# The inverse square root for x1, in the query-group loop: its Newton steps on GpSimd instead of VectorE

## The chip, the cores and the metric

One core of one Trainium2 chip runs the whole program. The metric is the device time of one execution in microseconds; lower is better.

## What is computed

The input x is [16, 16, 48, 128]: 16 batches of 768 tokens with 128 channels. Three blocks follow one another.

```
x = x + conv_attention(group_norm(x))          # 8 heads of 16, 768 x 768 scores, two biases, causal in t
t = t + additive_attention(layer_norm(t))      # tanh(A_i + B_j + b1), weighted by w2; softmax; times V
t = t + moe(layer_norm(t))                     # 8 experts, top 2, capacity 3840, gelu
layer_norm(v) = (v - mean(v)) / sqrt(var(v) + 1e-5)      # over the 128 channels of a token
```

The change is in the first `layer_norm`, that of x1 (the output of the first block). The kernel makes 1/sqrt(var + 1e-5) from a bit-trick seed and three Newton steps: y = y * (1.5 - 0.5 * var * y * y). A batch has 768 variances, held as 128 partitions x 6 numbers.

## The kernel before, in words

The work on batches is a software pipeline. Each batch goes through five stages (`STAGES`): pre (group norm, q, k, v), max (row maxima of the scores), mid (scores, weighted values, project, x1 and its layer norm), add (the additive attention) and end (second layer norm, gate, sending rows to experts). A pass holds one stage of each of up to five batches, and has 24 ticks. Pass p has batch p in add, p+1 in mid, p-1 in end. Passes -3 to 0 are written out, 1 to 12 are a hardware loop of two passes a turn (`passes`), 13 to 15 are written out again. The expert stage runs after all passes, from about 2090 us.

Every engine walks the same ticks in its own order of instructions, written out by hand; semaphores join them. TensorE, VectorE, ScalarE each have a `body(ps)`; the parts that matter here:

- **GpSimd** (`body`, L817): in tick q it first makes the sums of query group q (`sums`, L791): three instructions of 128x768 on `hidden` (L803), with a drain ahead of the second and third (ahead of the first too in ticks 7 to 18), the last of them raising `sums_ready`. It waits first for `logits_added` (L798), that is, until TensorE has used the `hidden` slot of four groups ago, and for group 0 for `ab_ready`. In ticks 18 to 23 and 0 to 5 it then sends one block of rows to the experts (`send`, L812: an indirect DMA whose descriptors GpSimd makes, L814).
- **ScalarE** (L889): in tick q it takes the exponentials of two score banks (L879), every fourth tick those of the logits (L886, which waits for VectorE's `logit_bias`), then waits for `sums_ready` of group q and takes the tanh of the sums (L902) and of a fourth part that it sums by itself (L906).
- **TensorE** (L1098): in tick q+1 it adds the logits of group q (`add_logits`, L978), fills score banks (L948, L951), weighs values (L964) and fills the three banks of `ring`: row maxima (L1052), and in ticks 20 and 21 the transposes of the normed x1 (L1037) and the products B and A (L1066), which wait for VectorE's copies of those transposes (L1291).
- **VectorE** (L1425): reads the ring banks in the order of their filling, and between the four slots of a tick has the small work. For x1: statistics in ticks 16 and 17; `norm_scale(0, k)` (L1205) with k = 0 (add 1e-5, seed: L1210, L1126) in tick 17 slot 2, and k = 1, 2, 3 (a Newton step each: L1129, L1131, L1133) in tick 17 slot 3 and tick 18 slots 1 and 3; then `normed` (L1216) for three blocks in tick 19 slot 1 and three in slot 3, which raises `x1n_ready`.

The same `norm_scale` serves the second layer norm (which = 1, ticks 4 to 6); the change leaves it.

## Time and profile before

| | |
|---|---|
| median of three runs | 2384.56 us (2372.84 to 2385.24) |
| the profiled execution | 2384.78 us, span 2383.0 us |
| TensorE busy | 2053.2 us, 86% of the span |
| VectorE busy | 1675.7 us, 70% |
| ScalarE busy | 1683.2 us, 71% |
| GpSimd busy | 1461.3 us, 61% |
| granted TensorE clock, mean | 0.951 of full speed |

The profiled execution took 1.8 us more than its span, and lies within 0.3 us of the median. The busy shares are averages over the passes and the expert stage. Semaphore waits and drains are not counted as busy; in the timelines they show as idle time ahead of an instruction, in brackets, with what ended it ("issue" when the profile shows no releaser).

### The profile page before, as it was taken

How to read it: one execution, taken by the hardware profiler on the slowest of the kernel's cores; microseconds unless marked ns; L12 is line 12 of the kernel's file. 1: busy time of each engine (PE TensorE's matmuls, PEld its weight loads, DVE VectorE, ACT ScalarE, POOL GpSimd, SP SyncE). 2: the span in 40 equal slices, each digit the busy share in tenths (PEclk: the TensorE clock that was granted, in tenths of full speed). 3: DMA queues.
4: the chain of work that ended last, by engine and by line, in shares of the span. 5: the costliest groups of instructions: out<-in, count | busy, mean ns of one | idle time of the engine just before them, and what ended most of it. 6: DMA issues, size and time to landing. Idle time of an engine off the chain costs nothing.

```text
span 2383.0 us, 56242 instructions
## 1 busy us (share of the span) xinstructions
PE 2053.2 (86%) x17665; PEld 1122.5 (47%) x17665; DVE 1675.7 (70%) x4534; ACT 1683.2 (71%) x1933; POOL 1461.3 (61%) x1525
## 2 busy tenths in 40 slices
PE   2889999989998999989998999999999977549986
PEld 1344444444444444444444444444444433338775
DVE  5787787787878787868786878787877665324433
ACT  5238787877887788778787878788878977613332
POOL 3006576656666656565666666666657877627777
PEclk7799999999999999999999999999999988869998
DMA  4546322322222223222323131313131000025553
GB/s 94 89 86 128 95 48 61 55 62 56 61 56 61 56 59 57 58 60 51 66 50 68 42 70 29 81 32 77 32 65 32 12 6 4 7 54 90 84 86 37
DMA packets 157499, 137.99 MB, mean 58 GB/s; under 512 B 24665, under 2 KB 149814, under 8 KB 157104
## 3 DMA queue, kind: packets, MB, share of 16 engines
q1 hardware_dynamic: 119376, 109.87, 22.5%
q0 software_dynamic: 23824, 16.85, 5.2%
q10 hardware_dynamic: 13968, 7.30, 1.2%
q8 instruction: 154, 2.52, 0.5%
q14 instruction: 177, 1.45, 0.2%
HBM read 82.68 MB, written 54.52 MB: 58 GB/s over the span
## 4 chain that ended last, share of the span: by engine, by line
PE 39%; DVE 22%; issue 13%; DVEq 9%; POOL 6%; ACT 4%; POOLq 3%; DMA 2%; SPq 0%; another core or an unknown queue 0%; ACTq 0%
PE logits L978 12%; DVE max_halves L1261 4%; POOL out_dram L583 4%; PE ring L1052 3%; PE av_bank L964 3%; POOLq L802 3%; PE ring L1074 3%; PE ring L1066 3%; PE scores L948 3%; PE scores L951 2%; ACT hidden L902 2%; DVE logit_bias L1447 2%; POOL hidden L803 2%; PE ring L1071 2%; DVEq L1448 2%
## 5 line engine op out<-in xcount | busy, mean ns | idle before, releaser
L803 POOL TENSOR_SCALAR hidden<-b_rep,a_cols 128x768 f32<-128x768 f32 x1152 | 1057.1, 920 | 765.6 <-issue 302.9
L902 ACT ACTIVATE hidden<-hidden 128x2304 f32<-128x2304 f32 x384 | 816.1, 2125 | 16.4 <-POOL hidden L803 16.4
L978 PE MATMUL logits<-hidden,w_shifted 128*32 128x384 f32 x6144 | 591.6, 504 | 65.3 <-ACT hidden L906 30.9
L879 ACT ACTIVATE probs<-scores 128x512 f32<-128x512 f32 (+1 forms) x768 | 391.9, 545 | 325.6 <-PE scores L951 320.9
L1261 DVE TENSOR_REDUCE max_halves<-ring 128x1 f32<-128x384 f32 (+4 forms) x896 | 471.3, 550 | 115.8 <-PE ring L1052 114.2
L906 ACT ACTIVATE hidden<-b_rep,a_cols 128x768 f32<-128x768 f32 x384 | 358.4, 933 | 0.0
L1052 PE MATMUL ring<-k_max,q_max 112*128 112x384 bf16 (+4 forms) x1024 | 296.0, 319 | 34.8 <-DVE max_halves L1261 25.9
L978 PEld LDWEIGHTS logits<-hidden,w_shifted 128*32 128x32 f32 x6144 | 164.0, 110 | 314.9 <-issue 246.7
L948 PE MATMUL scores<-bias_q,onehot_k 112*128 112x512 bf16 (+1 forms) x768 | 276.4, 360 | 4.8 <-ACT probs L879 1.8
L951 PE MATMUL scores<-q_parts,k_parts 98*128 98x256 bf16 (+1 forms) x1536 | 277.3, 262 | 0.0
L814 POOL DMA_INDIRECT expert_rows<-rows,slots x198 | 199.5, 1007 | 64.2 <-issue 32.7
L964 PE MATMUL av_bank<-probs,v_aug 128*32 128x256 f32 (+1 forms) x3072 | 224.8, 364 | 6.3 <-DVE headsT_raw L1433 6.1
L951 PEld LDWEIGHTS scores<-q_parts,k_parts 98*128 98x128 bf16 x1536 | 153.3, 100 | 116.8 <-issue 20.1
L1052 PEld LDWEIGHTS ring<-k_max,q_max 112*128 112x128 bf16 x1024 | 91.0, 99 | 245.2 <-issue 95.0
L886 ACT ACTIVATE probs<-logits,logit_bias 128x768 f32<-128x768 f32 x96 | 86.6, 902 | 132.7 <-DVE logit_bias L1449 127.9
L1074 PE MATMUL ring<-v,probs1T 128*128 128x128 f32 x1152 | 153.2, 284 | 21.8 <-DVE max_halves L1261 13.0
L1074 PEld LDWEIGHTS ring<-v,probs1T 128*128 128x128 f32 x1152 | 139.5, 195 | 41.4 <-DVE max_halves L1261 19.7
L510 ACT ACTIVATE hidden<-scores,eb1T 128x384 f32<-128x384 f32 x80 | 46.2, 581 | 132.2 <-PE scores L471 129.6
L1319 DVE COPY probs1T<-ring 128x384 f32<-128x384 f32 x192 | 102.6, 548 | 34.5 <-PE ring L1071 34.2
L964 PEld LDWEIGHTS av_bank<-probs,v_aug 128*32 128x32 f32 x3072 | 70.3, 109 | 103.8 <-issue 80.8
L482 PEld LDWEIGHTS logits<-probs,hidden 128*128 128x128 f32 x960 | 113.4, 192 | 12.1 <-issue 1.7
L482 PE MATMUL logits<-probs,hidden 128*128 128x128 f32 x960 | 113.7, 275 | 1.6 <-DVE gn_small L552 1.6
(262 smaller groups left out, 2585.8 us busy)
## 6 DMA issues: line engine op xcount, KB each, us to landing
qk_parts<-qk_parts_sb SPq DMA_DIRECT2D x16, 1152.0 KB, 4.7
q_parts<-qk_parts SPq DMA_DIRECT2D x192, 96.0 KB, 3.2
k_parts<-qk_parts SPq DMA_DIRECT2D x192, 96.0 KB, 4.3
q_max<-qk_parts SPq DMA_DIRECT2D x96, 96.0 KB
k_max<-qk_parts SPq DMA_DIRECT2D x96, 96.0 KB
expert_rows<-clear_row ACTq DMA_DIRECT2D x9, 792.0 KB, 5.0
x_in<-in_x_dram SPq DMA_DIRECT2D x96, 64.0 KB
x<-in_x_dram SPq DMA_DIRECT2D x96, 64.0 KB
```

The lines of the kernel that those rows point to most:

```text
L482: last = mm(logits[:, n % 2, P * b_:P * b_ + P], gelu_out[n % 2][:, j, P * b_:P * b_ + P], down_w[r][:, j, :], start=(j == 0), stop=(j == 3))
L803: last = g.tensor_scalar(hidden[:, q % SLOTS, o, :], b_rep[:, side], 1.0, a_cols[:, side, a_col(q, o):a_col(q, o) + 1], ALU.mult, ALU.add)
L879: s.activation(probs0[:, d % 3, 2 * pair:2 * pair + 2, 0:n_], scores[:, pair].rearrange("p (j l) -> p j l", j=2)[:, :, 0:n_], ACT.Exp) \
L902: s.activation(hidden[:, t % SLOTS, 0:3, :], hidden[:, t % SLOTS, 0:3, :], ACT.Tanh)
L906: s.activation(hidden[:, t % SLOTS, 3, :], b_rep[:, side], ACT.Tanh, bias=a_cols[:, side, col:col + 1]).then_inc(tanh_done, 1)
L948: mm(bank[:, :, 0:n_], onehot_k[:], bias_q[:, h:h + 2, q0 - P * kb:q0 - P * kb + n_], start=True, stop=False, skip_group_check=True)
L951: last = mm(bank[:, j, 0:n_], k_parts[0:98, h + j, P * kb:P * kb + P], q_parts[0:98, h + j, q0:q0 + n_], start=False, stop=True, skip_grou ...
L964: last = mm(av_bank[32 * g:32 * g + 32, q0 - lo:q0 - lo + n_], v_aug[:, side, kb, 4 * quad + g, :], probs0[:, d % 3, g, 0:n_], start=(kb = ...
L978: last = mm(logits[32 * g:32 * g + 32, half, 0:HALF], w2_shifted[:, k, :], hidden[:, q % SLOTS, g, HALF * half:HALF * half + HALF], start= ...
L1052: last = mm(bank[:, keys * j:keys * j + keys], q_max[:, h + j, P * qb:P * qb + P], k_max[:, h + j, lo:lo + keys], start=True, stop=True)
L1074: last = mm(bank[:, 0:P], probs1T[:, P * kb:P * kb + P], v1[:, ps.side(stage), kb, :], start=(kb == 0), stop=(kb == TB - 1))
L1261: v.tensor_reduce(max_halves[:, h:h + n_, part], bank[:, 0:n_ * keys].rearrange("p (h k) -> p h k", h=n_), AX.X, ALU.max, negate=True).the ...
```

## The change

GpSimd makes the three Newton steps for x1. VectorE still makes var + 1e-5 and the seed in tick 17, and the seed raises the new semaphore `x1_seeded`. GpSimd, in its tick 19, behind the three sums and ahead of the row send of that tick, waits for `x1_seeded` and issues twelve operations on 128x6 numbers, four to a step, with a drain between dependent ones; the last raises `x1_scaled`. VectorE waits for `x1_scaled` ahead of the first `normed` in tick 19, where it had a drain. VectorE's nine Newton operations and their drains are gone.

```
+SCALE_AT = 19
...
+            def norm_scale(ps):
+
+                var, y, tmp = (ln_small[:, 0, r, 0:TB] for r in range(3))
+                pool.wait_ge(x1_seeded, ps.batch("mid") + 1)
+                pool.sem_inc(pool_passed, 1)
+                for step in range(3):
+                    g.tensor_tensor(tmp, y, y, ALU.mult)
+                    pool.drain()
+                    g.tensor_tensor(tmp, tmp, var, ALU.mult)
+                    pool.drain()
+                    g.tensor_scalar(tmp, tmp, -0.5, 1.5, ALU.mult, ALU.add)
+                    pool.drain()
+                    last = g.tensor_tensor(y, y, tmp, ALU.mult)
+                    if step == 2:
+                        last.then_inc(x1_scaled, 1)
+                    else:
+                        pool.drain()
...
                     if ps.has("add"):
                         sums(ps, t)
+                    if t == SCALE_AT and ps.has("mid"):
+                        norm_scale(ps)
                     if ps.has("end"):
...
-                    rsqrt_seed(y, var)
+                    last = rsqrt_seed(y, var)
+                    if which == 0:
+                        last.then_inc(x1_seeded, 1)
...
-                            if t == 17 and slot >= 2:
-                                norm_scale(0, slot - 2)
-                            if t == 18 and slot in (1, 3):
-                                norm_scale(0, 2 + slot // 2)
-                            if t == 19 and slot in (1, 3):
-                                if slot == 1:
-                                    dve.drain()
-                                for tb in range(3 * (slot // 2), 3 * (slot // 2) + 3):
+                            if t == 17 and slot == 2:
+                                norm_scale(0, 0)
+                            if (t, slot) in ((19, 1), (19, 3)):
+                                half = slice(0, 3) if (t, slot) == (19, 1) else slice(3, 6)
+                                if half.start == 0:
+                                    dve.wait_ge(x1_scaled, ps.batch("mid") + 1)
+                                for tb in range(half.start, half.stop):
                                     last = normed(0, x1_, x1n, tb)
-                                if slot == 3:
+                                if half.start:
                                     last.then_inc(x1n_ready, 1)
```

GpSimd's instructions from tick 19 to tick 20 of a pass of the loop, before (L803 are the sums, L814 the row send, `x3` three in a row):

```order
99 L803 TENSOR_SCALAR hidden<-b_rep,a_cols 128x768 x3
100 L814 DMA expert_rows<-rows,slots 15360x132
101 L798 REGISTER_ALU
102 L803 TENSOR_SCALAR hidden<-b_rep,a_cols 128x768 x3
103 L814 DMA expert_rows<-rows,slots 15360x132
104 L798 REGISTER_ALU
```

and with the change (the sums are L806 there, the send L835; L816 to L822 are a Newton step):

```order
124 L806 TENSOR_SCALAR hidden<-b_rep,a_cols 128x768 x3
125 L813 REGISTER_ALU
126 L816 TENSOR_TENSOR ln_small<-ln_small 128x6
127 L818 TENSOR_TENSOR ln_small<-ln_small 128x6
128 L820 TENSOR_SCALAR ln_small<-ln_small 128x6
129 L822 TENSOR_TENSOR ln_small<-ln_small 128x6
...
137 L822 TENSOR_TENSOR ln_small<-ln_small 128x6
138 L835 DMA expert_rows<-rows,slots 15360x132
139 L801 REGISTER_ALU
140 L806 TENSOR_SCALAR hidden<-b_rep,a_cols 128x768 x3
```

Three such steps, twelve operations, stand between the sums of group 19 and the send of tick 19, so that send, the sums of group 20 and everything behind them stand behind the wait for the seed.

VectorE's own work on x1 from the seed (L1126) to the first normed blocks (L1217), before, in a pass of the loop; the reads of TensorE's banks and the second and third Newton step (but for its last row) are left out:

```order
685 L1210 TENSOR_SCALAR ln_small<-ln_mv 128x6
686 L1126 TENSOR_SCALAR ln_small<-ln_small 128x6
...
689 L1129 SCALAR_TENSOR_TENSOR ln_small<-ln_small 128x6
690 L1131 TENSOR_TENSOR ln_small<-ln_small 128x6
691 L1133 SCALAR_TENSOR_TENSOR ln_small<-ln_small 128x6
...
707 L1133 SCALAR_TENSOR_TENSOR ln_small<-ln_small 128x6
...
710 L1217 TENSOR_SCALAR heads<-x,ln_mv,ln_small 128x128 x3
```

and with the change, from the seed (L1149) on, with the reads of the banks, the names of semaphores waited for in brackets:

```order
667 L1233 TENSOR_SCALAR ln_small<-ln_mv 128x6
668 L1149 TENSOR_SCALAR ln_small<-ln_small 128x6
...
670 L1286 TENSOR_REDUCE max_halves<-ring 128x1 [waits ring_filled]
...
672 L1458 COPY headsT_raw<-av_bank 128x256 [waits av_done]
...
674 L1286 TENSOR_REDUCE max_halves<-ring 128x1 [waits ring_filled]
...
676 L1344 COPY probs1T<-ring 128x384 [waits ring_filled]
...
678 L1286 TENSOR_REDUCE max_halves<-ring 128x1 [waits ring_filled]
...
680 L1344 COPY probs1T<-ring 128x384 [waits ring_filled]
...
682 L1286 TENSOR_REDUCE max_halves<-ring 128x1 [waits ring_filled]
683 L1242 TENSOR_SCALAR heads<-x,ln_mv,ln_small 128x128 [waits x1_scaled]
684 L1242 TENSOR_SCALAR heads<-x,ln_mv,ln_small 128x128 x2
```

Between the seed and the normed blocks only the seven reads of TensorE's banks are left, and the first normed block waits for GpSimd.

## Rows read from the trace of the kernel before

**Rows 1.** Page, part 1: busy time, share of the span and instructions of each engine.
```profile
PE 2053.2 (86%) x17665; PEld 1122.5 (47%) x17665; DVE 1675.7 (70%) x4534; ACT 1683.2 (71%) x1933; POOL 1461.3 (61%) x1525
```

**Rows 2.** ScalarE in order of time, pass 7: start us, us, work [idle before <- releaser].
```profile
1134.50 2.15 ACT L902 ACTIVATE hidden<-hidden 128x2304 f32<-128x2304 f32 x1
...
1138.23 1.09 ACT L879 ACTIVATE probs<-scores 128x512 f32<-128x512 f32 x2 [0.76 <-PE scores L951]
1140.99 0.90 ACT L886 ACTIVATE probs<-logits,logit_bias 128x768 f32<-128x768 f32 x1 [1.67 <-DVE logit_bias L1449]
...
1141.89 2.11 ACT L902 ACTIVATE hidden<-hidden 128x2304 f32<-128x2304 f32 x1
```

**Rows 3.** GpSimd in order of time, pass 7, query groups 19 to 22.
```profile
1123.08 1.01 POOL L803 TENSOR_SCALAR hidden<-b_rep,a_cols 128x768 f32<-128x768 f32 x1 [0.17 <-issue]
1124.25 1.12 POOL L814 DMA_INDIRECT expert_rows<-rows,slots  x1 [0.16 <-issue]
1126.96 0.90 POOL L803 TENSOR_SCALAR hidden<-b_rep,a_cols 128x768 f32<-128x768 f32 x1 [1.59 <-PE logits L978]
1129.56 0.91 POOL L803 TENSOR_SCALAR hidden<-b_rep,a_cols 128x768 f32<-128x768 f32 x1 [1.70 <-issue]
1130.64 0.91 POOL L803 TENSOR_SCALAR hidden<-b_rep,a_cols 128x768 f32<-128x768 f32 x1 [0.17 <-issue]
...
1136.26 0.91 POOL L803 TENSOR_SCALAR hidden<-b_rep,a_cols 128x768 f32<-128x768 f32 x1 [2.61 <-issue]
1137.34 0.91 POOL L803 TENSOR_SCALAR hidden<-b_rep,a_cols 128x768 f32<-128x768 f32 x1 [0.17 <-issue]
...
1140.98 0.91 POOL L803 TENSOR_SCALAR hidden<-b_rep,a_cols 128x768 f32<-128x768 f32 x1 [0.58 <-issue]
```

**Rows 4.** VectorE in order of time, pass 7: seed, first scaled x1 blocks, copies of x1T.
```profile
1127.97 0.17 DVE L1126 TENSOR_SCALAR ln_small<-ln_small 128x6 int32<-128x6 int32 x1
...
1134.75 0.86 DVE L1217 TENSOR_SCALAR heads<-x,ln_mv,ln_small 128x128 f32<-128x128 f32 x3
...
1140.88 1.01 DVE L1291 COPY headsT<-ring 128x384 f32<-128x384 f32 x2
```

**Rows 5.** GpSimd by instruction group: busy us, mean ns | idle before, all of its run.
```profile
L719 POOL TENSOR_SCALAR_AFFINE_SELECT mask<-mask 128x8 f32<-128x8 f32 x2 | 0.4, 198 | 0.3
```

**Rows 6.** VectorE by instruction group: the nine x1 Newton operations of a pass.
```profile
L1129 DVE SCALAR_TENSOR_TENSOR ln_small<-ln_small 128x6 f32<-128x6 f32 x48 | 19.6, 408 | 4.4
...
L1131 DVE TENSOR_TENSOR ln_small<-ln_small 128x6 f32<-128x6 f32 x48 | 11.6, 242 | 3.6
...
L1133 DVE SCALAR_TENSOR_TENSOR ln_small<-ln_small 128x6 f32<-128x6 f32 x48 | 11.3, 236 | 3.9 <-issue 0.4
```

**Rows 7.** TensorE in order of time, pass 7, ticks 19 to 21.
```profile
1133.12 0.33 PE L1052 MATMUL ring<-k_max,q_max 112*128 112x384 bf16 x1
...
1139.43 0.64 PE L964 MATMUL av_bank<-probs,v_aug 128*32 128x256 f32 x8
...
1142.02 0.91 PE L1066 MATMUL ring<-headsT,map_b 128*128 128x384 f32 x2 [1.47 <-DVE headsT L1291]
```

**Rows 8.** GpSimd in order of time, pass 8, query groups 4 and 5.
```profile
1172.41 0.91 POOL L803 TENSOR_SCALAR hidden<-b_rep,a_cols 128x768 f32<-128x768 f32 x1 [3.58 <-issue]
...
1180.29 0.91 POOL L803 TENSOR_SCALAR hidden<-b_rep,a_cols 128x768 f32<-128x768 f32 x1 [3.79 <-issue]
```

**Rows 9.** ScalarE in order of time, pass 8, query group 6.
```profile
1187.60 2.13 ACT L902 ACTIVATE hidden<-hidden 128x2304 f32<-128x2304 f32 x1 [1.38 <-POOL hidden L803]
```

**Rows 10.** TensorE in order of time, pass 8, logits of query group 6.
```profile
1190.61 1.50 PE L978 MATMUL logits<-hidden,w_shifted 128*32 128x384 f32 x16 [1.28 <-ACT hidden L906]
```

**Rows 11.** Waits of ScalarE, whole run: us in total, times, longest us.
```profile
ACT hidden L902 <- POOL hidden L803: 16.4, 15, 2.7
```

**Rows 12.** GpSimd in order of time, first sums of pass 6, then of pass 9.
```profile
903.50 0.90 POOL L803 TENSOR_SCALAR hidden<-b_rep,a_cols 128x768 f32<-128x768 f32 x1 [1.96 <-PE logits L978]
...
1269.32 0.90 POOL L803 TENSOR_SCALAR hidden<-b_rep,a_cols 128x768 f32<-128x768 f32 x1 [2.57 <-PE logits L978]
```

More of the change, by code:

```diff
@@ L335, in hybrid_kernel @@
         x1n_ready = sem("x1n_ready")
+        x1_seeded = sem("x1_seeded")
+        x1_scaled = sem("x1_scaled")
         ab_ready = sem("ab_ready")
@@ L1125, in rsqrt_seed @@
             def rsqrt_seed(y, var):
-                v.tensor_scalar(y.bitcast(I32), var.bitcast(I32), -0.5, float(0x5F3759DF), ALU.mult, ALU.add)
+                return v.tensor_scalar(y.bitcast(I32), var.bitcast(I32), -0.5, float(0x5F3759DF), ALU.mult, ALU.add)
             def rsqrt_step(y, var, tmp):
```

## The prediction

> **What bounds the kernel now.** I began with the busy shares [rows 1]: TensorE leads with 86%, VectorE and ScalarE have 70 and 71%, GpSimd 61%. By these GpSimd has room. They are averages, so I went to the timelines of one pass, around the ticks that the change touches.
>
> ScalarE in ticks 17 to 20 of pass 7 has no idle time: its tanh of group 20 starts at 1134.50 the moment its work before ends. Behind it there are only 0.76 us of idle for scores and 1.67 us for VectorE before the tanh of group 21 at 1141.89 [rows 2]. GpSimd [rows 3] ends the sums of group 19 at 1123.08 + 1.01 = 1124.09, issues a row send, and runs the sums of group 20 from 1126.96 to 1130.64 + 0.91 = 1131.55. That is 2.95 us before ScalarE wants them. The reader should then see that GpSimd does not rest again. Its brackets say "issue", and they stand ahead of the second sum, where the drain waits for the send before it: 1.70, 2.61 and 0.58 us. Sums, send, sums, send run end to end from group 20 into group 6 of the next pass. There the drains take 3.58 and 3.79 us [rows 8], and ScalarE waits 1.38 us for group 6 [rows 9], TensorE 1.28 us for that tanh [rows 10]. So the engine with the third-lowest load sets the pace once per pass; ScalarE waits 15 times for it, 16.4 us in all [rows 11].
>
> VectorE's seed for x1 ends at 1127.97 + 0.17 = 1128.14, the first normed block starts at 1134.75 [rows 4].
>
> **The change, part by part.**
>
> *VectorE.* The nine operations cost 19.6 + 11.6 + 11.3 = 42.5 us and 11.9 us of gaps over 16 batches [rows 6]: 54.4 us, 3.4 us a batch. What of it is on the path? From the seed to the first normed block VectorE reads banks that TensorE fills: the last maxima before that block start at 1133.12 and take 0.33 [rows 7], so with a read of half a microsecond (two copies of that size take 1.01 [rows 4]) that block can start at about 1134.0 instead of 1134.75. ScalarE sets the pace there. The next VectorE work that TensorE waits for is the copy of x1T [rows 4], for 1.47 us [rows 7]; half a microsecond of that could come back, if nothing else is late. It is, as shown below. I take 2 us for the whole run; the ends are 0 and 16 x 0.7 = 11 us.
>
> *The wait on GpSimd.* GpSimd is through with group 19 at 1124.09 and must stand until 1128.14, about 1128.3 with the signal. That is 4.2 us. Behind it on GpSimd are the send and all sums from group 20 on; ScalarE waits for those.
>
> *The twelve operations.* No row has a GpSimd operation of this form. Nearest is the 128x8 select in the setup, 198 ns and 0.15 us of gap for its drain [rows 5]; the gap ahead of a drained sum is 0.17 [rows 3]. The low end is 0.25 us each (3.0 in all), if plain arithmetic is shorter than a select. The high end is 0.58 (7.0 in all): VectorE's first operation of a step averages 408 ns, its third 236 [rows 6], so something holds up operations of this size; 0.41 + 0.17 is what as much would make here. I take 0.33, near the select: 4.0 us. The block ends at 1132.3, ahead of the 1134.0 of the normed block, so VectorE does not wait; it would from 0.48 us each on.
>
> *The sum on GpSimd in pass 7.* 1132.3, then the send 0.16 + 1.12, then the sums of group 20, 1131.55 - 1126.96 = 4.59 with the drain's 1.70. They end at about 1138.2: 6.6 us later, 3.7 us after ScalarE wants them. The send and the sums of group 21, with a short drain of 0.6 as the send at that time of the pass has now [rows 3], add 1.28 + 3.49 = 4.77: 1142.95 instead of 1137.34 + 0.91 = 1138.25, a delay of 4.7 us.
>
> *What ScalarE's lateness costs at once.* The tanh that start at 1134.50 end 0.75 us before the exponentials of 1138.23; 3.7 us late, those exponentials start at 1141.2 and end at 1142.3. TensorE's value products at 1139.43 [rows 7] need them and go at 1142.4. Behind the products (0.6) stand the second transposes of x1 (an estimate of 0.6, as the products) and VectorE's copy (0.5), so the matmuls that started at 1142.02 start at about 1144.1: 2.1 us.
>
> *What the delay costs later.* The 4.7 us run down GpSimd's unbroken row of sums and sends. Three of the passes of the loop (3, 7, 11) go into the next without a wait, and there the sums of group 4 end at 1172.41 + 0.91 + 0.17 + 0.91 = 1174.40 [rows 8], 0.25 us before ScalarE wants them: 4.5 us each, 13.4. After four passes (1, 5, 9, 10) GpSimd waits 1.5 to 2.0 us at the first sums of the next, as at 903.50 [rows 12], which absorbs that much: 2.9 each, 11.7. After passes 2, 4, 8 and 12 it waits 2.57 and more [rows 12], so only the immediate 2.1 is left: 8.4. Pass 6 has 4.45 us of room at group 20, not 2.95; I put it at 1, and the passes outside the loop (0, 13, 14), with fewer or no sends, at 1 together.
>
> Sum: 13.4 + 11.7 + 8.4 + 2 - 2 = +33.5 us on the profiled execution of 2384.8. That execution is the median (2384.6) to within 0.3 us. **2418 us.**
>
> One rule speaks for a smaller cost. The row shows that a drain after a send takes 1.70 us with VectorE's small operations around it and 0.58 us later [rows 3]. The Trainium skill, "SBUF — State Buffer", section "SBUF: two separate sides", says that VectorE operations in a two-port mode lock GpSimd out of the shared ports, so that it cannot write the descriptors of its sends. By it, fewer VectorE operations on SBUF could shorten the drain of group 20 from 1.7 to 0.6; with that the sum would be some 12 x 1.1 = 13 us less, 2405. No row separates the nine operations from the normed blocks that also stand there, so the sum keeps 1.7.
>
> **The rivals.**
>
> *Only the first wait counts.* The drains shrink as the row of sends moves away from VectorE's work on x1 and x2: the 3.58 and 3.79 [rows 8] belong to that time. Then group 6 is no later than before, and a pass costs 0.5 to 1.5 us: +7 to +20, 2392 to 2405. For it: the drains of 1.70 and 2.61 against 0.58 two sends later [rows 3]. Against it: VectorE moves along with TensorE, so its work comes later too.
>
> *GpSimd's small operations are dear.* At 0.58 us each the block is 7.0 us, 3 us more; the normed blocks wait as well (x1_scaled at 1135.3 against 1134.0). Each microsecond here lies on the row in about 12 passes: 33 + 36 = +69, 2454. For it: VectorE's 408 against 236 ns [rows 6]. Against it: the sums of 0.91 us stretch by 0.1 at most [rows 3].
>
> *VectorE's relief wins: faster.* The place is the copy of x1T, where TensorE waits 1.47 us [rows 7]. If the sums of group 20 still come in time, up to 0.7 us a pass come back: 16 x 0.7 = 11, and with shorter stalls beside it up to 20 us: 2365 to 2373. This decides from the point where GpSimd's delay at group 20 is below the slack of 2.95. The wait for the seed takes 4.2 by itself, the operations at least 3.0, and what the pause ahead of group 20 gives back is 1126.96 - 1124.25 - 1.12 = 1.6. 5.6 against 2.95 even at the low end; only a drain of 0 instead of 1.7 and operations of 0.1 us would do it.
>
> *Nothing measurable.* Lateness at group 20 is swallowed by ScalarE's 0.76 + 1.67 us of idle [rows 2], and group 6 catches up. It needs a lateness below 2.4, and the sum says 3.7.
>
> **How the numbers follow.** The chain as worked out, +20 to +50: 0.57. Only the first wait: 0.20, a third of it within 12 us. Dear operations: 0.11. Nothing measurable: 0.07. Faster: 0.05. A measurement of this kernel can tell about 0.5%, 12 us, from no change. Slower by more than that: 0.57 + 0.13 + 0.11 = 0.81; within it: 0.07 + 0.07 = 0.14; faster 0.05. The range takes in the chain, nearly all of "only the first wait" and most of the dear operations: 2391 to 2448.
>
> **What would show it.** GpSimd's first Newton operation starts at the seed's end in every pass of the loop, 4 us after its sums; twelve operations end about 4.0 us later. VectorE's normed blocks wait for nothing on GpSimd, and start up to 0.7 us sooner after the seed. ScalarE waits for the sums of group 20 for about 3.7 us in some 12 passes, where it waited in none, and again at groups 4 to 6; its waits for GpSimd grow from 16 us to some 60. VectorE's busy time falls by about 42 us, and nothing is gained by it. The forecast is wrong if ScalarE's tanh of group 20 still follows its work before without idle time, or if the operations end after the normed blocks could have started.

## The result, and the profile after

The changed kernel takes **2397.70 us** (median of 20 runs, 2386.07 to 2403.60) against 2383.98 us for the kernel before, measured beside it (20 runs, 2368.00 to 2389.16). The ratio is 1.0061, with a 95% interval of 1.0045 to 1.0076: slower by 14 us. The forecast was 2418, slower by 34; its direction was right and its size two and a half times too large. The profiled execution took 2397.37 us (span 2395.5).

The busy times of the page, after, answer to [rows 1] (PE is TensorE, PEld its weight loads, DVE VectorE, ACT ScalarE, POOL GpSimd):

```profile
PE 2062.3 (86%) x17665; PEld 1121.7 (47%) x17665; DVE 1625.4 (68%) x4390; ACT 1680.3 (70%) x1933; POOL 1502.4 (63%) x1717
```

VectorE lost 144 operations (nine in each of 16 batches) and 50.3 us of busy time; GpSimd gained 192 operations and 41.1 us. GpSimd in order of time, pass 7, answers to [rows 3] (start us, us, work, idle before):

```profile
1129.69 0.91 POOL L806 TENSOR_SCALAR hidden<-b_rep,a_cols 128x768 f32<-128x768 f32 x1 [0.17 <-issue]
1135.27 0.20 POOL L816 TENSOR_TENSOR ln_small<-ln_small 128x6 f32<-128x6 f32 x1 [4.67 <-DVE ln_small L1149]
1135.61 0.20 POOL L818 TENSOR_TENSOR ln_small<-ln_small 128x6 f32<-128x6 f32 x1
...
1139.10 0.20 POOL L822 TENSOR_TENSOR ln_small<-ln_small 128x6 f32<-128x6 f32 x1
1139.84 1.03 POOL L835 DMA_INDIRECT expert_rows<-rows,slots  x1 [0.53 <-issue]
1140.93 0.91 POOL L806 TENSOR_SCALAR hidden<-b_rep,a_cols 128x768 f32<-128x768 f32 x1
1143.37 0.92 POOL L806 TENSOR_SCALAR hidden<-b_rep,a_cols 128x768 f32<-128x768 f32 x1 [1.53 <-issue]
1144.45 0.91 POOL L806 TENSOR_SCALAR hidden<-b_rep,a_cols 128x768 f32<-128x768 f32 x1 [0.17 <-issue]
```

The sums of group 19 are done at 1130.60; GpSimd stands 4.67 us for the seed, the twelve operations run from 1135.27 to 1139.30 (4.03 us), and the sums of group 20 end at 1145.36. ScalarE, same pass, answers to [rows 2]:

```profile
1145.39 2.13 ACT L925 ACTIVATE hidden<-hidden 128x2304 f32<-128x2304 f32 x1 [2.97 <-POOL hidden L806]
...
1149.20 0.90 ACT L909 ACTIVATE probs<-logits,logit_bias 128x768 f32<-128x768 f32 x1
...
1150.24 2.12 ACT L925 ACTIVATE hidden<-hidden 128x2304 f32<-128x2304 f32 x1
...
1155.40 2.13 ACT L925 ACTIVATE hidden<-hidden 128x2304 f32<-128x2304 f32 x1 [1.67 <-POOL hidden L806]
```

The tanh of group 20 now waits 2.97 us for its sums. But the pauses that stood behind it before, 0.76 us for scores and 1.67 us for `logit_bias` [rows 2], are gone: from the tanh of 20 to that of 21 it is 4.85 us, where it was 1141.89 - 1134.50 = 7.39. The waits of the whole run say the same (us in all, times, longest). Before, where not shown yet:

```profile
ACT probs L879 <- PE scores L951: 320.9, 230, 48.2
...
ACT probs L886 <- DVE logit_bias L1449: 127.9, 72, 9.4
...
PE ring L1037 <- DVE heads L1217: 21.2, 15, 6.1
```

and after, the second row answering to [rows 11]:

```profile
ACT probs L902 <- PE scores L974: 232.5, 171, 48.9
...
ACT hidden L925 <- POOL hidden L806: 166.5, 86, 5.6
...
ACT probs L909 <- DVE logit_bias L1474: 91.0, 64, 4.2
...
PE ring L1060 <- DVE heads L1242: 8.4, 15, 2.2
```

ScalarE's waits for GpSimd grew by 150 us; its waits for TensorE's scores and VectorE's `logit_bias` fell by 88 + 37 = 125. By these sums most of the new wait took the place of waits that were there.

Where in a pass the time goes shows best in a table that I worked out from the tanh rows of ScalarE: the start of each tanh counted from that of group 17 of the same pass, mean of passes 1 to 11, as the difference from the kernel before, in us. The last column is the length of a pass less that of before. Each line is one profiled execution, and not always one near its kernel's median: that of e4 was 9 us faster than its median, those of e6 and e9 (below) 14 and 13 us faster, that of e13 11 us slower. e1 to e4 are experiments below.

```
group                   20    21    22    23     0     2     3     4     5     6     9    17
before, us            11.5  19.6  23.3  30.4  34.4  47.4  51.2  54.8  62.1  66.6  85.4 122.3
after                 +3.4  +0.4  +1.7  +0.1  +1.2  -0.9  +1.3  +4.4  +2.2  +2.5  +1.8  +2.0
e1 no steps           +0.1  -0.5  -0.6  -0.7  -0.7  -0.7  -0.6  -0.6  -0.3  +0.2  +0.3  +0.7
e2 wait and twelve    +3.5  +0.4  +1.9  +0.1  +1.4  -0.5  +2.5  +5.1  +3.0  +3.2  +2.5  +2.3
e3 wait alone         -0.1  +0.9  +1.3  +1.8  +1.8  +1.6  +1.7  +2.0  +2.1  +2.0  +1.9  +1.7
e4 twelve alone        0.0  +1.1  +1.6  +2.4  +2.4  +2.0  +2.1  +2.1  +2.2  +2.1  +2.0  +1.5
```

The 3.4 us at group 20 are given back at 21 all but 0.4. The price comes at groups 3 and 4 of the next pass, and 1.8 to 2.0 us of it stay. GpSimd itself, counted in the same way, ends the sums of group 20 6.4 us later than before and those of group 6 3.3 us later: in between it runs without a rest and regains 3.0.

The table covers passes 1 to 11 only. Over all passes the change is 21.8 us late at the last tanh (2085.61 against 2063.84), and 9.3 us of that are given back behind it, where the last batch and the experts are left: 309.9 us instead of 319.2. GpSimd begins to send the last batch's rows 31.8 us after the last tanh, where the kernel before needs 38.7. The experiments have both lengths too: 310 to 311 us in e1 to e4, e9 and e11 to e14, 318 in e5 to e8, 314 in e10. What decides between them no run shows, so it stays open whether the change has a part in it.

### The profile page after: what moved, and what is told of

Read it like the earlier page. It is cut to its first block, busy times and chain, and to the rows that moved or that the text cites. A ratio compares the mean times of both kernels' runs of the same rounds, so it can differ in the third digit from the quotient of the medians.

```text
span 2395.5 us, 56328 instructions
## 1 busy us (share of the span) xinstructions
PE 2062.3 (86%) x17665; PEld 1121.7 (47%) x17665; DVE 1625.4 (68%) x4390; ACT 1680.3 (70%) x1933; POOL 1502.4 (63%) x1717
## 4 chain that ended last, share of the span: by engine, by line
PE 33%; issue 18%; DVE 15%; POOLq 11%; POOL 11%; DVEq 5%; ACT 4%; DMA 2%; SPq 1%; ACTq 0%
PE logits L1001 11%; POOLq L805 10%; POOL hidden L806 7%; POOL out_dram L586 4%; PE av_bank L987 3%; DVE max_halves L1286 3%; PE ring L1097 3%; PE ring L1075 2%; PE scores L971 2%; PE scores L974 2%; DVE logit_bias L1472 2%; PE ring L1066 2%; ACT hidden L925 1%; DVEq L1473 1%; PE ring L1094 1%
## 5 line engine op out<-in xcount | busy, mean ns | idle before, releaser
L806 POOL TENSOR_SCALAR hidden<-b_rep,a_cols 128x768 f32<-128x768 f32 x1152 | 1061.3, 923 | 514.7 <-issue 292.7
L925 ACT ACTIVATE hidden<-hidden 128x2304 f32<-128x2304 f32 x384 | 815.6, 2124 | 166.8 <-POOL hidden L806 166.5
L1001 PE MATMUL logits<-hidden,w_shifted 128*32 128x384 f32 x6144 | 602.4, 511 | 71.2 <-ACT hidden L929 36.4
L902 ACT ACTIVATE probs<-scores 128x512 f32<-128x512 f32 (+1 forms) x768 | 386.1, 541 | 234.8 <-PE scores L974 232.5
L835 POOL DMA_INDIRECT expert_rows<-rows,slots x198 | 199.1, 1006 | 63.4 <-issue 38.8
L816 POOL TENSOR_TENSOR ln_small<-ln_small 128x6 f32<-128x6 f32 x48 | 9.4, 197 | 202.3 <-DVE ln_small L1149 197.7
L971 PEld LDWEIGHTS scores<-bias_q,onehot_k 112*128 112x128 bf16 x768 | 76.2, 99 | 101.0 <-issue 49.0
```

Source lines behind the costliest of these rows:

```text
L806: last = g.tensor_scalar(hidden[:, q % SLOTS, o, :], b_rep[:, side], 1.0, a_cols[:, side, a_col(q, o):a_col(q, o) + 1], ALU.mult, ALU.add)
L902: s.activation(probs0[:, d % 3, 2 * pair:2 * pair + 2, 0:n_], scores[:, pair].rearrange("p (j l) -> p j l", j=2)[:, :, 0:n_], ACT.Exp) \
L925: s.activation(hidden[:, t % SLOTS, 0:3, :], hidden[:, t % SLOTS, 0:3, :], ACT.Tanh)
L971: mm(bank[:, :, 0:n_], onehot_k[:], bias_q[:, h:h + 2, q0 - P * kb:q0 - P * kb + n_], start=True, stop=False, skip_group_check=True)
L1001: last = mm(logits[32 * g:32 * g + 32, half, 0:HALF], w2_shifted[:, k, :], hidden[:, q % SLOTS, g, HALF * half:HALF * half + HALF], start= ...
```

## The experiments

Fourteen kernels were run, in four rounds on four chips, each with the kernel before beside it (medians 2381.79, 2381.96, 2380.17 and 2379.54 us). Line numbers in the rows are those of each kernel. The theories at the start were CHAIN, that of the prediction (GpSimd's delay is paid in full at groups 20 and 4 to 6, VectorE's relief is worth about nothing), with SLACK (ScalarE's own waits absorb the delay) and RELIEF (what VectorE no longer does gives back some 20 us of CHAIN's price) against it.

### Taking the change apart: e1 to e4

e1 is the change without any Newton step (x1 is scaled by the seed alone); VectorE does not wait for GpSimd, and GpSimd does what it did before:

```
-                    if t == SCALE_AT and ps.has("mid"):
-                        norm_scale(ps)
...
-                                    dve.wait_ge(x1_scaled, ps.batch("mid") + 1)
+                                    dve.drain()
```

> VectorE's nine Newton operations for x1 are left out and GpSimd does nothing in their place: x1 is scaled by the seed alone (the three Newton steps are not computed). Theory RELIEF (the forecast's +34 us of GpSimd delay is there, and VectorE's relief gives some 20 back): about 20 us faster than before, 2364. Theory SLACK (the relief is worth what the prediction said, and the delay of GpSimd is mostly absorbed): 0 to 5 us faster, 2379 to 2384.

e2, e3 and e4 are the kernel before, with all its steps on VectorE, and on GpSimd at the change's place the wait for the seed, the twelve operations on a tile of their own, or both:

```
+            def spare_scale(ps):
+                pool.wait_ge(x1_seeded, ps.batch("mid") + 1)      # e2, e3
+                var, y, tmp = (spare[:, r, :] for r in range(3))  # e2, e4, with the twelve operations
...
```

> VectorE keeps its Newton steps; GpSimd waits for the seed in tick 19 and makes the same twelve operations on a spare tile. GpSimd is as late as in the change, VectorE has no relief. RELIEF: +34 us against before, 2418, and 20 more than the change. SLACK: about +14 to +19, 2398 to 2403, no more than 5 above the change.

> VectorE keeps its Newton steps; GpSimd only waits for the seed behind the sums of group 19. The sums of group 20 then end about 4.2 - 1.6 = 2.6 us later than before, inside the 2.95 us that ScalarE leaves them. Both theories: no wait of ScalarE at group 20. If the delay itself runs down the row of sums and sends: +10 to +20 us through groups 4 to 6. SLACK: within 5 us of before.

> VectorE keeps its Newton steps; GpSimd makes twelve operations of 4.0 us on a spare tile behind the sums of group 19, without waiting for the seed. They fill the pause of 1124.09 to 1128.3, so the sums of group 20 are 4.0 - 1.6 = 2.4 us late at most, inside the slack. As for the wait alone: within 5 us of before by SLACK, +10 to +20 if the delay runs down the row. If it equals the wait alone, wait and operations cost only together, once they pass 2.95 + 1.6 us.

| | median us | ratio to before | interval |
|---|---|---|---|
| e1 no steps | 2370.24 | 0.9955 | 0.9931 to 0.9979 |
| e2 wait and twelve | 2404.36 | 1.0089 | 1.0055 to 1.0122 |
| e3 wait alone | 2396.87 | 1.0075 | 1.0048 to 1.0102 |
| e4 twelve alone | 2399.06 | 1.0070 | 1.0035 to 1.0104 |

By the ratios, leaving VectorE's steps out gains 10.7 us (0.45%), where the prediction took 2. The delay of GpSimd costs 21 us with VectorE's work unchanged, where it took 35.5. Together +10, beside the measured +14: within the intervals the change is these two, added. Both fell between the theories: e1 gained more than SLACK's 0 to 5 us and less than RELIEF's 20, e2 came out just above SLACK's 2398 to 2403 and far from RELIEF's 2418, and e3 and e4 lie outside SLACK's 5 us.

Where e1 gains is another matter. In its trace passes 1 to 11 are each 0.7 us longer than before, although group 21 comes 0.5 us earlier. It is 4.9 us ahead when they begin, 3.0 behind when they end, and gains 8.3 in passes 12 to 15 and 8.5 behind the last tanh, where e2 to e4, without any relief, gain 8.2 to 9.4 as well. So the relief is shown for the run as a whole, not for the place where it was looked for.

The surprise is e3 and e4. Each costs 17 to 18 us, nearly as much as both together, and yet ScalarE waits for GpSimd no more than before (19.4 us in all in e3, 17.6 in e4, [rows 11] had 16.4). By the table their loss starts at group 21, not 20. The groups of VectorE's normed blocks of x1 show it (busy us, mean ns | idle before). Before, and with the wait alone:

```profile
L1217 DVE TENSOR_SCALAR heads<-x,ln_mv,ln_small 128x128 f32<-128x128 f32 x96 | 43.0, 503 | 1.5
```

```profile
L1230 DVE TENSOR_SCALAR heads<-x,ln_mv,ln_small 128x128 f32<-128x128 f32 x96 | 56.3, 642 | 1.5
```

Of the two halves of pass 7, three operations each, the first took 0.86 us before [rows 4], the second:

```profile
1137.82 1.00 DVE L1217 TENSOR_SCALAR heads<-x,ln_mv,ln_small 128x128 f32<-128x128 f32 x3
```

With the wait alone, VectorE in order of time, pass 7:

```profile
1136.90 1.94 DVE L1230 TENSOR_SCALAR heads<-x,ln_mv,ln_small 128x128 f32<-128x128 f32 x3
...
1141.39 2.09 DVE L1230 TENSOR_SCALAR heads<-x,ln_mv,ln_small 128x128 f32<-128x128 f32 x3
```

and GpSimd beside them:

```profile
1136.49 1.00 POOL L823 DMA_INDIRECT expert_rows<-rows,slots  x1 [0.15 <-issue]
1137.54 0.97 POOL L807 TENSOR_SCALAR hidden<-b_rep,a_cols 128x768 f32<-128x768 f32 x1
...
1141.12 1.00 POOL L823 DMA_INDIRECT expert_rows<-rows,slots  x1 [0.15 <-issue]
1142.17 0.98 POOL L807 TENSOR_SCALAR hidden<-b_rep,a_cols 128x768 f32<-128x768 f32 x1
```

The three operations of a half take 0.34 us each where they run alone. Here the first of each half ends 0.35 us after the send, the second 0.08 us after the sum, and they took 0.93 and 0.85 us in the first half, 1.07 and 0.85 in the second: they stood while GpSimd worked. VectorE's statistics of x and its maxima of the ring keep their 0.29 and 0.55 us beside a sum. The Trainium skill, "SBUF — State Buffer", section "SBUF: two separate sides", states this as an exclusive lock of a port pair between GpSimd's operations and those of VectorE that use two ports or two sources in SBUF; by that rule, the trace agrees. It does not show the rule to the last step, since the second operation needs 0.34 us alone and ends 0.08 us after the sum.

How this reaches group 21 the rows of all passes tell. In each of passes 1 to 11 of the kernel before, of e3 and of e4, the tanh of group 21 starts 3.05 to 3.07 us after the end of the last of the six blocks, whatever came before. With the wait alone the six operations take 4.0 us of a pass instead of 2.7 (passes 1 to 11); they start 0.5 us earlier than before and end 1.0 us later. So a GpSimd operation moved by 2 to 4 us lands on other VectorE work and makes that late. In the change itself the 3.07 us hold in four passes only; in the other seven it is 4.1 to 4.7, and the late ScalarE sets group 21. TensorE waits for the blocks 32.7 us in the whole of e3, 31.9 in e4, 21.2 before.

### Which wait is it: e5 to e8

Two theories were left: LAG (GpSimd's lateness from group 20 to 6) and that of the blocks (NORM, PORT, later LOCK in the texts below). e5 is the change with the twelve operations on a tile of their own and no wait on VectorE (x1 is scaled by the seed alone); e6 moves one send:

```
-                    if t == SCALE_AT and ps.has("mid"):
-                        norm_scale(ps)
                     if ps.has("end"):
...
                                     send(m)
+                    if t == SCALE_AT and ps.has("mid"):
+                        norm_scale(ps)
```

> The changed kernel, but GpSimd makes its twelve operations on a spare tile and VectorE doesn't wait for them before the normed blocks of x1; the Newton steps are left out of the computation (the seed alone is used). GpSimd still waits for the seed and its sums of group 20 and after are as late as in the change. Theory LAG (the price is GpSimd's lateness, which it carries from group 20 to group 6 of the next pass, running back to back): as the change, 2394 to 2401 us, a median of +13 over the kernel before. Rival JOIN (the price is VectorE's wait for the result in tick 19): 2380 to 2388, near the kernel before or under it.

> The change with one thing moved: GpSimd's row send of tick 19 is issued ahead of its Newton block, while it would wait for the seed anyway, and not behind it. The twelve operations keep their times; the sums of group 20 and all behind them come some 1.4 us earlier. Theory LAG: what is left of the lateness at group 6 is 1.4 us less in each of twelve passes, 2382 to 2390 us, 8 to 15 less than the change. Rival NORM (what counts is when the normed blocks and the copies behind them let tick 21 begin, which stays where it is): 2394 to 2400, as the change.

e7 and e8 place the row sends by a table; e7 is the change with the Newton block behind them, e8 the kernel before. The cut shows the two tables; the waits for sent rows and the drains ahead of sums are fitted to them, and with e8 there is a drain ahead of the first sum of group 0 where there was none:

```
+SEND_NOW = {17: (0,), 18: (1,), 19: (2, 3, 4), 20: (5,), 21: (6,), 22: (7,), 23: (8,)}   # e7
+SEND_NEXT = {0: (9,), 1: (10,), 2: (11,)}
+SEND_NOW = {17: (0,), 18: (1,), 19: (2,), 20: (3,), 21: (4,), 22: (5,), 23: (6,)}        # e8
+SEND_NEXT = {0: (7,), 1: (8,), 2: (9,), 3: (10,), 4: (11,)}
```

> The change with the twelve row sends of a batch placed otherwise: one each in ticks 17 and 18, three in tick 19 ahead of the Newton block (where GpSimd waits for the seed), one each in ticks 20 to 23 and 0 to 2 of the next pass; so seven fall into the stretch from tick 20 to tick 5 and not ten as in the change (with its send of tick 19 behind the block eleven). Theory LAG: GpSimd has caught up before tick 6 and ScalarE's waits for its sums fall from 167 us to under 80; the time is the relief of VectorE with little against it, 2368 to 2380 us. Rival NORM: 2390 to 2400. Rival PORT (sums that land beside the normed blocks and the Newton steps hold VectorE up, wherever the sends are): 2385 to 2395.

> The kernel before (all Newton steps on VectorE) with the row sends one each in ticks 17 to 23 and 0 to 4, a tick earlier than they were. GpSimd's lead at ticks 5 and 6 grows from some 1 us to 2; ScalarE waited only 16 us for its sums in all. Theory LAG: 2372 to 2384 us, a gain of 0 to 10. Rival PORT: sums shift against VectorE's normed blocks either way, 2375 to 2400 with the same waits for GpSimd.

| | median us | ratio to before | interval | ScalarE's waits for GpSimd, us |
|---|---|---|---|---|
| e5 no wait on VectorE | 2409.30 | 1.0106 | 1.0073 to 1.0138 | 183.7 |
| e6 send first | 2390.69 | 1.0034 | 1.0009 to 1.0058 | 45.2 |
| e7 sends moved, after | 2403.48 | 1.0085 | 1.0056 to 1.0114 | 57.4 |
| e8 sends moved, before | 2403.05 | 1.0072 | 1.0045 to 1.0099 | 7.7 |

VectorE's wait for the result is not the price: without it the kernel is 11 us slower still. Why it is slower I can't say; the trace shows that the late form of groups 1 to 4 (over 22 us from the tanh of 1 to that of 5, for what takes 18 to 19) stands in 8 of passes 1 to 11, in the change in 7, and that 7.8 of the 16 us between the two profiled executions lie behind the last tanh. The time is above LAG's 2394 to 2401 as well. e6 gains 7 us on the change, just short of LAG's 8 to 15, and lies 3 us under NORM's 2394. e7 and e8 went against LAG: the waits for GpSimd fell as wanted, to a third of the change's and to half of before's, and the time rose by 17 to 21 us on before. NORM and PORT, whose upper ends were 2400 and 2395 for e7 and 2400 for e8, missed too, by 3 to 9 us. In e8 GpSimd does the work of the kernel before at other moments, and the loss is again at group 21 (+0.6) and 23 (+1.6). There one normed operation takes 1.77 us in five of passes 1 to 11: it begins during a send and ends 0.08 us after the sum behind it. TensorE waits 27.5 us for the normed blocks.

### The clock behind group 20

The windows from the tanh of group 20 to those of 21, 22 and 23 show the rest. Columns: stretch, length, busy us of each engine with its instructions, the granted clock of TensorE, DMA share, GB/s. The engines stand in the order TensorE, its weight loads, VectorE, ScalarE, GpSimd. Before, pass 7 and then pass 4:

```profile
1134.50:1141.89 7.39, 5.76 (x53) 3.21 (x49) 6.38 (x22) 4.96 (x8) 4.68 (x5) 1.00 0.05 14
1141.89:1145.25 3.36, 3.23 (x20) 1.69 (x24) 1.67 (x3) 3.36 (x6) 2.82 (x3) 1.00 0.17 46
1145.25:1151.87 6.62, 6.62 (x67) 3.68 (x63) 3.70 (x9) 4.04 (x5) 4.80 (x6) 1.00 0.03 10
```

```profile
761.87:770.86 8.99, 6.32 (x53) 3.40 (x49) 7.99 (x22) 4.96 (x8) 6.37 (x7) 0.88 0.09 20
770.86:775.19 4.33, 4.20 (x11) 2.41 (x12) 1.24 (x2) 3.49 (x7) 3.41 (x5) 0.50 0.12 36
775.19:783.04 7.85, 7.85 (x73) 3.96 (x75) 4.14 (x9) 4.02 (x5) 2.84 (x4) 0.98 0.04 12
```

In pass 4 the copies of x1's halves are 1.6 us later, TensorE stands 2.67 us of the first window instead of 1.63, and its granted clock falls to 0.50 of full speed, the lower of its two levels (1.2 GHz), for the whole of group 21. Groups 21 and 22 then take 12.18 us instead of 9.98. Of passes 1 to 11 the clock is below 0.9 in the window of group 21 in 5 before, in 8 in e3, 9 in e4, 8 in e8. In the kernel before, e3, e4 and e8 every pass whose clock stayed at 1.00 there takes 9.98 or 9.99 us from the tanh of 21 to that of 23, and every pass whose clock fell takes 11.5 to 13.4. So of the 1.8 us by which e3 is late at group 23, 0.9 come from the blocks and are there at 21, the rest comes with the clock.

How long TensorE stood does not decide alone whether the clock falls. Pass 1 of the kernel before is nearly pass 7 (TensorE stands 1.69 us of the first window), and its clock falls:

```profile
395.82:403.27 7.45, 5.76 (x53) 3.21 (x49) 6.45 (x22) 4.97 (x8) 4.67 (x5) 1.00 0.08 23
403.27:407.45 4.18, 4.05 (x12) 2.11 (x12) 1.21 (x3) 3.48 (x6) 2.88 (x4) 0.59 0.14 37
```

In passes 6 and 8 it stands 2.44 and 2.54 us, and the clock stays at 1.00. What makes it fall is open. The change itself, pass 7:

```profile
1145.39:1150.24 4.85, 3.11 (x23) 1.61 (x22) 3.40 (x11) 4.80 (x7) 3.79 (x4) 1.00 0.05 17
1150.24:1155.40 5.16, 5.16 (x46) 2.06 (x49) 2.86 (x6) 3.49 (x5) 3.74 (x4) 1.00 0.10 29
1155.40:1160.13 4.73, 4.73 (x50) 3.12 (x46) 3.17 (x7) 3.92 (x5) 3.74 (x4) 1.00 0.04 14
```

Here the clock falls at group 21 in only 2 of the 11 passes. It is no gain over the whole pass, because with the change the clock falls at another place, groups 4 and 5. Pass 7, from the tanh of 4 to those of 5 and 6:

```profile
1189.97:1194.66 4.69, 1.20 (x5) 0.64 (x6) 2.19 (x7) 4.69 (x7) 3.75 (x4) 0.82 0.14 43
1194.66:1199.73 5.07, 5.07 (x34) 1.70 (x36) 1.75 (x6) 3.92 (x6) 3.74 (x4) 0.50 0.06 17
```

TensorE worked 1.20 of 4.69 us and then ran at the lower level. This happens in 7 of the 11 passes, the same seven that have the late form of groups 1 to 4; it happens in 8 passes of e2 and 9 of e5, in none of the kernel before, e1, e3 and e4. The mean granted clock of the whole run is 0.948 with the change, 0.951 before.

### Doses and places: e9 to e12

e9 is e6 with two steps on GpSimd; e10 the kernel before with two steps on VectorE; e11 the change with SCALE_AT = 20; e12 the change with six steps:

```
-                for step in range(3):
+                for step in range(2):            # e9; range(6) in e12
...
-                            if t == 18 and slot in (1, 3):
-                                norm_scale(0, 2 + slot // 2)
+                            if t == 18 and slot == 1:       # e10
+                                norm_scale(0, 2)
```

> The change with the row send of tick 19 ahead of the Newton block and two Newton steps on GpSimd in place of three (eight operations; the inverse root of x1 then has two steps in all, the third is left out). The sums of group 20 come 2.5 us earlier by the send and 1.3 by the step than in the change, 2.5 us later than in the kernel before. Theory LAG (the price is what is left of GpSimd's lateness at groups 3 to 6): it has caught up by then, and the relief of VectorE is left: 2370 to 2382 us. Rival LOCK (VectorE's normed blocks of x1 stand still while a sum runs beside them, and tick 21 starts when the copies behind them are done): the sums now fall on the blocks, tick 21 starts 0.5 to 1.5 us later than in the kernel before, 2386 to 2398.

> The kernel before with two Newton steps for x1 on VectorE in place of three, nothing on GpSimd (the third step is left out). A third of the relief that the kernel without steps had (10.7 us): theory LAG 2376 to 2382. Rival LOCK: the normed blocks start 0.7 us earlier and meet GpSimd's sums in another way, 2370 to 2400, and the time goes with the length of the six normed operations (3.0 us a batch before, 3.9 with the wait alone), not with the steps.

> The change with the Newton block one tick later, behind the sums of group 20: GpSimd no longer waits for the seed (it was made some 3.5 us before), the sums of group 20 are on time, those from 21 on 4.0 us late, and the result comes some 3 us later, so that VectorE waits with the normed blocks and the ring reads behind them. Theory LAG: a third less lateness at groups 3 to 6, but tick 21 starts 1 to 2 us later since the copies of x1's halves are late: 2392 to 2405 us. Rival SEED (the price of the change is the 2.4 us that GpSimd stands waiting for the seed beyond where it would go on): 2380 to 2390.

> The change with six Newton steps on GpSimd in place of three (the result is the same; twelve operations and 4.0 us more per batch): the normed blocks and the sums of group 20 come 4.0 us later than in the change. Theory LAG, with no slack left anywhere from group 20 to 6: nearly all of it is paid in each of twelve passes, 36 to 48 us on the change, 2433 to 2446. Rival ABSORB (ScalarE's own waits for TensorE and VectorE behind group 20 take up most of a delay, however long): 8 to 20 on the change, 2405 to 2418.

| | median us | ratio to before | interval | clock fell at group 21, of 11 passes |
|---|---|---|---|---|
| e9 send first, two steps | 2385.23 | 1.0017 | 0.9988 to 1.0046 | 4 |
| e10 two steps, on VectorE | 2358.91 | 0.9900 | 0.9872 to 0.9927 | 0 |
| e11 block in tick 20 | 2385.60 | 1.0027 | 0.9994 to 1.0060 | 6 |
| e12 six steps | 2455.88 | 1.0311 | 1.0263 to 1.0360 | 8 |

e12 tells how far a delay is absorbed. It costs 58 us on the change. In the trace its block takes 8.4 us where the change's takes 4.04, and passes 1 to 11 are 3.9 us longer each than the change's; 10 of the 61 us between the two profiled executions lie ahead of these passes, 8 behind them. VectorE now waits 38.1 us in all for the result (16 times), and the clock falls at group 21 in 8 passes. So the change, with VectorE's relief, costs 2.0 us in each of passes 1 to 11, and 4.4 us more of GpSimd work cost 3.9: what absorbs is nearly used up by then. LAG's 36 to 48 was too little for the run, though not for these passes, and ABSORB's 8 to 20 is out. e11 tells what the wait for the seed is worth. The block takes the same time, but GpSimd does not stand for the seed first, and ScalarE's waits for its sums are 20.8 us in all: 2385.6 us, not to be told from no change, within SEED's 2380 to 2390 and under LAG's 2392 to 2405. VectorE has its relief there too, so this is not the price of the wait by itself. e9 lies 3 us above LAG's upper end and just below LOCK's lower one; its normed operations average 600 ns, as LOCK had it, with little lateness left.

e10 is the fastest, 21 us under the kernel before (24 by the ratio), and under both forecasts, LAG's 2376 and LOCK's 2370. Its windows of pass 4:

```profile
754.92:762.37 7.45, 5.43 (x49) 2.92 (x48) 6.54 (x19) 4.96 (x8) 6.18 (x7) 1.00 0.03 11
762.37:765.73 3.36, 3.23 (x20) 1.69 (x24) 1.67 (x4) 3.36 (x6) 2.60 (x4) 1.00 0.16 46
765.73:772.35 6.62, 6.62 (x67) 3.67 (x63) 3.70 (x9) 4.04 (x5) 3.47 (x5) 1.00 0.04 13
```

In all eleven passes the clock stays at 1.00 at group 21, and from the tanh of 21 to that of 23 it is 9.99 us. TensorE stands up to 2.54 us of the first window here too. Passes 1 to 11 together are 10.1 us shorter than before; 3.9 of the gain lie ahead of them, 11.8 in passes 12 to 15 and 5.1 behind the last tanh. By the ratios one step less gains 24 us, and three steps less (e1) only 10.7; the clock had fallen in 4 passes of e1.

### Work or moment: e13, e14

e13 keeps all three steps on VectorE, one slot earlier each; e14 has one step:

```
-                            if t == 17 and slot >= 2:         # e13
-                                norm_scale(0, slot - 2)       # e13
-                            if t == 18 and slot in (1, 3):    # e13, e14
-                                norm_scale(0, 2 + slot // 2)  # e13, e14
+                            if t == 17 and slot >= 1:         # e13
+                                norm_scale(0, slot - 1)
+                            if t == 18 and slot == 1:
+                                norm_scale(0, 3)
```

> The kernel before with all three Newton steps on VectorE, each one slot earlier: seed in slot 1 of tick 17, steps in slots 2 and 3 of it and in slot 1 of tick 18, nothing in slot 3 of tick 18; nothing is left out, and nothing moves to GpSimd. Theory GATE (what counts is whether TensorE stands so long between ticks 20 and 21, behind the normed blocks and copies of x1, that its granted clock falls for ticks 21 and 22; it fell in 5 of 11 passes before and in none with two steps): with slot 3 of tick 18 free the blocks come as early as with two steps, no or few passes fall, 2355 to 2368 us. Rival WORK (the gain of the two-step kernel is the work left out): the work is the same as before, 2376 to 2386.

> The kernel before with one Newton step for x1 on VectorE (two steps are left out of the computation). Theory WORK (the gain goes with the operations left out: 21 us for one step): 2335 to 2355 us. Theory GATE (the time goes by the passes in which the clock falls behind tick 20, which depends on where GpSimd's sums meet the normed blocks): not below the two-step kernel by more than 4, 2355 to 2380 us, as the kernel without steps was slower (2370) than the one with two (2359).

e13: 2405.59 us, ratio 1.0098 (1.0062 to 1.0134). e14: 2366.48 us, 0.9949 (0.9931 to 0.9966).

e14 lies in GATE's range and outside WORK's: the gain does not go with the work left out (by the ratios one step left out 24 us, two 12, three 11). e13 went against both theories. In its trace the steps one slot earlier make the tanh of group 20 itself 1.7 us late and that of 21 1.9, so the blocks did not come earlier at all. A likely cause, not shown: VectorE's small operations in slots 1 and 2 of tick 17, each behind a drain, stand in front of reads of the ring that ScalarE's scores hang on. Which read it is I did not follow further. So that the clock explains e10's gain is argued from the rows; the run that was to show it with all the work kept did not move the blocks as meant. With all steps kept, no kernel here beats the one before. **The best version is e10**, 1.0% under the kernel before and 1.6% under the change (2358.91 against 2397.70, on different chips), but it leaves the third Newton step for x1 out, and whoever uses it has to want that.

## Why the prediction was right or wrong

- **The twelve operations, 4.0 us a batch: right.** 0.20 us each and 0.15 for the drain behind it, 4.03 in pass 7, where 0.33 each was taken. The block begins 0.18 us after the seed. "Dear operations" is out; VectorE's 408 ns [rows 6] come from standing beside GpSimd, not from the operation, which takes 0.17 us where GpSimd does nothing.
- **The wait for the seed, 4.2 us: right in size** (4.67 in pass 7; in the loop 4.04 and 4.67 in turn).
- **Sums of group 20 6.6 us late, ScalarE 3.7: right.** 6.4 and 3.4 in the mean.
- **"What ScalarE's lateness costs at once", 2.1 us: this step failed.** In the sum it is the term of 8.4. It followed the exponentials, value products and copies as if all of them had to come after the late tanh. Measured, the tanh of group 21 is 0.4 us late in the mean, in e2 too, which has no relief. Before, the copies of x1's halves set it (3.07 us behind the normed blocks in every pass), and those hang on VectorE, not on the tanh of 20; the pauses of 0.76 and 1.67 us were cover and were used up. The rival "nothing measurable" named these pauses, and was turned down by comparing 3.7 with 2.4 as if the row had no more room than two brackets of one pass.
- **"What the delay costs later": the place right, the size too large.** ScalarE does wait for the sums of groups 3, 4 and 6, and the price shows at groups 3 and 4. The prediction's start, that GpSimd sets the pace once per pass, was too strong: behind passes 1 to 11 ScalarE waited for it nine times before, six of them at group 6. All terms of the delay together were 35.5 us, and e2, which has the delay alone, measured 21. Pass by pass the split can't be checked. Passes 3, 7 and 11, taken at 4.5 us each, grew by 3.5, 6.1 and 2.7 (tanh of group 12 to that of the next pass), a mean of 4.1; passes 2, 4 and 8, taken at 2.1, by 2.2, 0.1 and 3.4; passes 1, 5, 9 and 10, taken at 2.9, by +2.8, -1.7, -1.6 and +4.8, a mean of 1.1. That looks like a hit for the first kind, but e1, whose GpSimd is not late, grew by 3.9, 6.2 and 3.9 in the same passes 3, 7 and 11 and by -1.2 and 0.4 in the mean of the other two kinds. The clock of the kernel before had fallen at group 21 in passes 1, 2, 4, 5 and 9 and not in 3, 7 and 11, so another kernel tends to look worse in those three.
- **VectorE's relief, 2 us: too small by a factor of five.** e1 measured 10.7, the high end that the prediction itself gave (11). The prediction took ScalarE as pacing that stretch, where it is the chain over normed blocks and copies. But that the relief is earned there is not shown: passes 1 to 11 of e1's trace have no gain, and two steps left in gain more than none.
- **Nothing was said of the stretch behind the last tanh**, where 9.3 of the 21.8 us are given back in the two traces.
- **The rule on the ports** was used for the sends' drain only. The drain ahead of the second sum of group 20 went from 1.70 to 1.53 us, not to 0.6: that reading of it brought nothing. What the rows show is the other way round, GpSimd's sums and sends holding VectorE's blocks.
- **Signs foretold:** VectorE's busy time fell by 50 us (42 forecast), the normed blocks start about 6.0 us after the seed instead of 6.6 in pass 7 (6.6 instead of 6.8 in the mean of passes 1 to 11), ScalarE waits for groups 20 and 3 to 6, and for 22, 23 and 0 besides, 166.5 us in all and not 60. That number alone would have suggested a far larger loss; 125 us of it replaced other waits.

What stays open: why the change without VectorE's wait is slower than with it, what makes the clock fall at group 21 in one pass and not in the next, and where the two lengths behind the last tanh come from. The stretched blocks and the clock were separated by no run of their own. That the blocks make group 21 late and the clock groups 21 and 22 longer is read from the rows, pass by pass; a kernel whose blocks GpSimd can't hold was not tried.

## What to carry to other kernels

When an engine is made late, add up the delay only to the first place where its consumer waits for someone else anyway: there it is given back, up to that wait and no further (the change cost 2.0 us in each of passes 1 to 11, 4.4 us more of GpSimd work another 3.9). Moving an operation between GpSimd and VectorE also moves every later GpSimd operation against VectorE's, and where they meet can cost as much as the delay. Look at the granted clock in every window of a pass, not only where the change was made: here it fell less often at group 21 and in 7 of 11 passes at groups 4 and 5, where the trace of before has no fall. And do not check a forecast pass by pass against a single execution of the kernel before, whose own good and bad passes then pass for an effect.

## What the runs showed of the hardware

One of VectorE's normed operations, 128x128 numbers from and to SBUF, takes 0.34 us alone and mostly 0.85 to 1.08 when it is held by a GpSimd sum or row send beside it, ending 0.08 us after a sum and 0.35 after a send. It can be held through more than one: 1.77 us through a send and a sum (e8, e9), once 3.36 through a send and three sums (before, at 1959.4 us). Reductions and statistics were not held. Where TensorE's granted clock fell in the window of group 21 (mean 0.50 to 0.60), the way from the tanh of 21 to that of 23 took 11.5 to 13.4 us, otherwise 9.98 or 9.99 (before, e3, e4, e8, passes 1 to 11). The same kernel's runs spread with the clock: among 29 runs of the kernel before, the fastest (2363.59 us) had a mean granted clock of 0.958 and the slowest (2398.00) one of 0.944, more than the 14 us in question.
